# Reciprocal standard deviation of a node update: square root on ScalarE and a Newton step on VectorE in place of GpSimd's power

## The reference, cut to what matters

```
y = concatenate(h, agg);  x1 = x + h + silu(y @ uW1 + ub1) @ uW2 + ub2
h2 = (x1 - mean(x1)) / sqrt(var(x1) + 1e-5)
logits = h2 @ router_w.T            # top 2 of 8 experts, softmax, shares
out = x1 + h2 + sum of share * expert(h2)
```

## Time and profile before

| what | value |
|---|---|
| median of 3 runs | 2668.64 us (2668.3 to 2669.28) |
| the profiled execution's own time | 2669.72 us |
| its span in the profile | 2668.0 us |
| busy share of the span: PE, PEld, DVE, ACT, POOL | 76, 70, 79, 63, 66% |
| ACT_TABLE_LOAD instructions on ACT | 4, one each at L506, L1095, L1549, L1915 |
| the update's first instructions, last send | 2149.95 us, 2379.46 us |

### The profile page before, as it was taken

How to read it: one execution, slowest core, us unless ns; L and a number is a source line. 1 busy time by engine, 2 the same in 40 slices (tenths; PEclk the granted TensorE clock), 3 DMA queues, 4 the chain that set the end, 5 groups by cost and what they waited for, 6 DMA issues and landing times. The chain is left out here.

```text
span 2668.0 us, 63199 instructions
## 1 busy us (share of the span) xinstructions
PE 2024.5 (76%) x14160; PEld 1864.0 (70%) x14161; DVE 2099.9 (79%) x6765; ACT 1692.9 (63%) x3817; POOL 1769.8 (66%) x2247
## 2 busy tenths in 40 slices
PE   0000595009999999999999999999999979829980
PEld 0000584008999999999999999999999857719980
DVE  9994474028999999999999999999999837736766
ACT  5340121027888888888888888888888735418860
POOL 0007777738887878878878788788788715755660
PEclk9999998558999999999999999999999989959995
DMA  5000243012222222222222222222222354444548
GB/s 162 0 0 9 73 144 94 6 37 76 72 72 71 73 71 71 74 71 71 73 72 72 73 70 73 71 71 74 71 71 73 65 172 128 143 127 132 155 134 290
DMA packets 145565, 230.56 MB, mean 86 GB/s; under 512 B 33241, under 2 KB 101491, under 8 KB 145214
## 3 DMA queue, kind: packets, MB, share of 16 engines
q0 software_dynamic: 60672, 139.93, 18.0%
q1 hardware_dynamic: 75758, 81.69, 10.2%
q10 hardware_dynamic: 9040, 7.85, 0.9%
HBM read 167.41 MB, written 61.73 MB: 86 GB/s over the span
## 5 line engine op out<-in xcount | busy, mean ns | idle before, releaser
L1035 POOL DMA_INDIRECT rows<-b_rows,dst_row x838 | 841.9, 1005 | 229.9 <-issue 146.7
L1162 PE MATMUL ps_z<-w_hi,t_hi 128*128 128x256 f32 x1676 | 547.3, 327 | 0.0
L1149 PE MATMUL ps_agg<-rows,onehot 128*126 128x256 f32 x1676 | 453.8, 393 | 19.6 <-DVE node_rows L1184 16.6
L1163 PE MATMUL ps_z<-w_lo,t_hi 128*128 128x256 f32 x1676 | 468.3, 279 | 0.0
L1164 PE MATMUL ps_z<-w_hi,t_lo 128*128 128x256 f32 x1676 | 467.9, 279 | 0.0
L1068 ACT ACTIVATE rows<-rows,shift,rstd_m 128x256 f32<-128x256 f32 x838 | 452.5, 587 | 0.0
L1184 DVE TENSOR_TENSOR node_rows<-node_rows,ps_agg 126x256 f32 x838 | 345.2, 412 | 105.5 <-issue 88.6
L460 POOL DMA_INDIRECT sorted_edges<-pay,place x245 | 241.9, 987 | 279.3 <-DVE place L802 199.5
L1095 ACT ACTIVATE rows<-rows 128x512 f32<-128x512 f32 x419 | 265.0, 632 | 188.4 <-DVE rows L1240 181.8
L1149 PEld LDWEIGHTS ps_agg<-rows,onehot 128*126 128x126 f32 x1676 | 281.3, 187 | 75.6 <-DVE node_rows L1184 25.3
L1045 POOL TENSOR_TENSOR rstd_m<-mv_m,half_m 128x2 f32<-128x2 f32 x419 | 307.2, 733 | 34.9
(11 more groups left out here) (316 smaller groups left out, 4366.3 us busy)
## 6 DMA issues: line engine op xcount, KB each, us to landing
x_e<-by_expert SPq DMA_DIRECT2D x56, 260.0 KB, 2.9
rows<-b_rows,dst_row POOLq DMA_INDIRECT x838
y_back<-y_rows SPq DMA_DIRECT2D x49, 252.0 KB
b_rows<-b_out SPq DMA_DIRECT2D x50, 126.0 KB
u_rows<-u_out SPq DMA_DIRECT2D x50, 126.0 KB
xh_rows<-xh_out SPq DMA_DIRECT2D x50, 126.0 KB
u_row_up<-u_rows SPq DMA_DIRECT2D x50, 126.0 KB
xh_row_up<-xh_rows SPq DMA_DIRECT2D x50, 126.0 KB
```

Of the source, the lines that this page charges most:

```text
L1035: nc.gpsimd.indirect_dma_start(rows[r][:, i, :], None, dram["b_rows"], bass.IndirectOffsetOnAxis(ap=dst_row[:, r, i:i + 1], axis=0)).then_ ...
L1149: mm = pe.matmul(ps_agg[0:BIN, i * D:(i + 1) * D], onehot[:, q, i, 0:BIN], rows[q][:, i, :], start=True, stop=True)
L1162: pe.matmul(z, t_hi[:, k, i, c, :], w2_hi[:, c, :], start=(c == 0), stop=False)
L1163: pe.matmul(z, t_hi[:, k, i, c, :], w2_lo[:, c, :], start=False, stop=False)
```

## The change

POOL's two operations per pair of bins go. ACT takes the square root of variance plus epsilon in the same even step, after its Silu, with epsilon as a bias that POOL sets once. DVE makes the reciprocal of the root and refines it by one Newton step, five chained operations, in the odd step before the normalization that uses it. `mv` keeps the variance without epsilon, so the one later use (`gain`) adds it.

```
-            nc.gpsimd.memset(half[:], -0.5).then_inc(consts, 1)
+            nc.gpsimd.memset(eps[:], LN_EPS).then_inc(consts, 1)
...
-            def normal(g):
-                hold(pool, stats_ready, g + 2)
-                nc.gpsimd.tensor_scalar(mv[0:BIN, g:g + 2, 1], mv[0:BIN, g:g + 2, 1], 1.0, LN_EPS, ALU.mult,
-                                        ALU.add).then_inc(eps_added, 1)
-                pool.wait_ge(eps_added, g // 2 + 1)
-                nc.gpsimd.tensor_tensor(rstd[0:BIN, g:g + 2], mv[0:BIN, g:g + 2, 1], half[0:BIN, :], ALU.pow
-                                        ).then_inc(rstd_ready, 1)
...
             for n in range(STEPS):
-                if due(n - 6) and n % 2 == 0:
-                    normal(n - 6)
...
                     nc.scalar.activation(act1[0:BIN, g % R, :], act1[0:BIN, g % R, :], ACT.Silu
                                          ).then_inc(silu_ready, 1)
+                g = n - 6
+                if due(g) and g % 2 == 0:
+                    if g == 0:
+                        act.wait_ge(consts, 12)
+                    act.wait_ge(stats_ready, g + 2)
+                    nc.scalar.activation(root[0:BIN, g:g + 2], mv[0:BIN, g:g + 2, 1], ACT.Sqrt, bias=eps[0:BIN, 0:1]
+                                         ).then_inc(root_ready, 1)
...
+            def normal(g):
+                y, var = rstd[0:BIN, g:g + 2], mv[0:BIN, g:g + 2, 1]
+                a, b = newton[0:BIN, 0, :], newton[0:BIN, 1, :]
+                dve.wait_ge(root_ready, g // 2 + 1)
+                then(nc.vector.reciprocal(y, root[0:BIN, g:g + 2]))
+                then(nc.vector.tensor_tensor(a, y, y, ALU.mult))
+                then(nc.vector.scalar_tensor_tensor(out=b, in0=var, scalar=LN_EPS, in1=a, op0=ALU.add, op1=ALU.mult))
+                then(nc.vector.tensor_scalar(a, b, -0.5, 1.5, ALU.mult, ALU.add))
+                nc.vector.tensor_tensor(y, y, a, ALU.mult).then_inc(rstd_ready, 1)
...
                 g = n - 7
                 if due(g):
+                    if g % 2 == 0:
+                        normal(g)
                     dve.wait_ge(rstd_ready, g // 2 + 1)
...
-            then(nc.vector.tensor_tensor(gain[0:BIN, :], mv[0:BIN, :, 1], rstd[0:BIN, :], ALU.mult))
+            then(nc.vector.scalar_tensor_tensor(out=gain[0:BIN, :], in0=mv[0:BIN, :, 1], scalar=LN_EPS,
+                                                in1=rstd[0:BIN, :], op0=ALU.add, op1=ALU.mult))
```

More of the change, by code:

```diff
@@ L1273, in update @@
         rstd = sb("rstd_u", [P, BINS])
-        half = sb("half_u", [P, 2])
+        eps = sb("eps_u", [P, 1])
+        root = sb("root_u", [P, BINS])
+        newton = sb("newton_u", [P, 2, 2])
         blank = sb("blank", [P, E, 2, XROW])
@@ L1322, in update @@
         stats_ready = sem("stats_ready")
-        eps_added = sem("eps_added")
+        root_ready = sem("root_ready")
         consts = sem("consts_u")
```

## The result

The median goes from 2668.47 us (4 runs, 2664.75 to 2669.28) to 2681.76 us (4 runs, 2680.26 to 2683.56): 13.3 us slower, a ratio of 1.0052, with a 95% interval of 1.0041 to 1.0064.

What follows compares the result with a forecast made beforehand. PE's order and its waits for ACT and DVE were taken to bound the stage; 19.3 us lost less 7.6 from POOL gave 11.7 on 2669.7, 2681.4 profiled, so 2680 median. Own range 2674 to 2690, widened to 2669 to 2693.

Steps and rivals of the forecast that it cites:

- What bounds the stage: Update loop: PE's order and its waits for ACT's `agg_t`/`act_t` and DVE's normalization, 0.27 us to spare, set the step.
- ACT's part: ACT: 47 more table loads of about 1.3 us; `agg_t` 0.3 us late, 0.8 in 16 steps with a weight copy.
- The load back: ACT, odd step: load before Silu, which ends 2.64 us after `agg_t` began; next `agg_t` wanted at 2.93, so covered.
- the rival of 2711: ACT: each table switch costs twice the load, 2.7 to 3.2 us a pair, giving 2711 us; chance 0.07.
- DVE's part: DVE, odd step: five chained operations take 1.05 us (0.85 to 1.3), so `ps_ht` comes 0.78 us late.
- Both meet in one step: Odd steps: PE waits for the later delay, not the sum; 18.3 us for 23 pairs plus 1.0 in routing steps, 19.3.
- What POOL gives back: Relief from POOL's dropped work in landing-row waits, tail and final sends: 7.6 us together.
- The 2.0 for landing rows: Loop: ACT's waits for first sends to land before renaming rows vanish; 2.0 us of their 6.4 counted.
- The tail's relief of 3.0: Tail steps: waits for POOL's power and the rename go, two Newton chains and a load come; 3.0 us net, 1 to 5.
- for that I had 2.6: End of stage: POOL would owe no sends beyond the 25 after the last batch of five is placed; 2.6 us gained.
- The sum: Whole kernel: 19.3 - 7.6 = 11.7 us on the profiled 2669.7, giving 2681.4; median predicted 2680.

Runs made afterwards that it cites:

- no_switch_ht: Changed kernel with Identity for Sqrt on ACT, Newton chain kept, and PE's transposition of the normalized rows one step later: 2670.86 us, ratio 1.0012.
- neither: Changed kernel with Identity for Sqrt on ACT and the reciprocal alone on DVE, so no table loads and no Newton step: 2668.41 us, ratio 0.9989.
- no_newton: Changed kernel with the reciprocal alone on DVE, without the four Newton operations; Sqrt and its table loads stay: 2682.24 us, ratio 1.0046.
- newton_twice: Changed kernel with a second Newton step on DVE, nine chained operations in place of five: 2709.5 us, ratio 1.0155.
- no_switch: Changed kernel with Identity in place of Sqrt on ACT, so no table load; the Newton chain on DVE stays: 2687.39 us, ratio 1.0059.

## Why the prediction came out, step by step

It said 2680.0 us, between 2669 and 2693; measured 2681.76.

**What bounds the stage** held. PE's order of work and the two results that it waits for, `act_t` and the normalized rows, decide, and idle time of ACT or DVE elsewhere in the step counts for nothing. no_switch_ht shows it from the other side: the same operations on DVE, with another place to be ready for, cost a fraction.

**ACT's part** held with small errors. 47 loads came, of 1.283 us, each switch without a standstill beside the load. Sqrt on two columns took 0.295 us, not the logits copy's 0.18. That makes `agg_t` 0.1 us later than I had said, 0.9 late in place of 0.8 in step 35, which follows a step of the kind that I had read. In most other steps behind a weight copy it is 1.15 late, as in the timeline above, because there `agg_t` is wanted 0.93 us after Silu's end and not 1.18 as in the earlier trace rows: I had priced 16 steps from one. The load back is hidden, as said: Silu ends 2.64 us after `agg_t` began (2300.51 to 2303.15), the figure of the prediction. The switch alone costs 13.0 us in 21 odd steps (84.58 against 71.54); by my lateness (15 with a weight copy at 0.8, 6 at 0.3) it would be 13.8.

The Trainium skill ("ScalarE: Activation LUTs", What ACT_TABLE_LOAD costs) states about 2.66 us for every switch, half of it a drain. The trace differs: from Silu's end to Sqrt's start, with the load between, it shows 1.30 us (2298.43 to 2299.73), and the measurement decides. By the page's figure the rival of 2711 would have been near; it is refuted.

**DVE's part** held: 0.97 us for the chain, where I had taken 1.05 between 0.85 and 1.3. Four more operations cost 0.80 more. The root is ready long before, as said.

**Both meet in one step** held, and is the step that carries the result: chain alone +18.6 us of loop (3.3 of it clock), switch alone +12.1, both +17.2 rather than 30.7. I had 18.3 for 23 pairs, 16.7 of it for the 21 whose odd steps lie in the loop, and 1.0 for routing steps; the odd steps measured +19.3 and the even ones -2.1. Behind a weight copy I had put the two delays 0.02 us apart; the chain is the longer in 9 of the 15 odd steps behind one.

**What POOL gives back** is the term that I mis-sized: 7.6 us predicted, and some 3.4 seen. Without chain and switch the medians leave 2.7 us (2671.14 to 2668.41). The 2.0 for landing rows came: the waits are gone from the loop, in after as in neither. Neither's whole loop of 144.4 us doesn't show it, since the clock fell in steps 11 and 12 and other odd steps are up to 0.2 us longer, but single steps do. In before ACT waits for landing rows in steps 27, 32, 37, 42 and 47; of the steps behind them, 33, 38, 43 and 48 take 3.53, 3.05, 3.52 and 3.35 us in before and 3.12, 2.67, 3.07 and 2.67 in neither, 1.9 us less, and 28 is unchanged. The tail's relief of 3.0 came to 0.7: in neither the tail is 3.3 us shorter than before's, in no_newton 3.1, and with the whole chain 0.7 (0.8 of what is missing is step 51, which I had among the pairs). And POOL still owed sends when the last batch of five was placed; for that I had 2.6, and 0.8 came. These are the places, and the last two sends (the code leaves 25 after the places):

```profile
2363.21 0.17 DVE L1683 CAST place_up<-place_f_up 126x10 int32<-126x10 f32 x1
...
2396.30 0.99 POOL L1447 DMA_INDIRECT by_expert<-node_rows,place_up  x1 [0.30 <-issue]
2397.59 1.14 POOL L1447 DMA_INDIRECT by_expert<-node_rows,place_up  x1 [0.30 <-issue]
```

That is 35.5 us where 25 sends at 1.29 make 32.3: some two sends were owed, as before (in both traces 27 sends start behind the places). I had said that POOL, freed and in longer steps, would owe none. But POOL can send only what has been placed: the batch ahead of it was placed at 2351.99, 11.2 us earlier, and the ten sends that this released, from 2352.99 on, take 12.9; ahead of them POOL had stood idle for 4.75 us. In the tail the places come faster than the sends, whatever POOL did earlier. The counter-example is newton_twice: with its tail 4.0 us longer, only the 25 sends start behind the places, and they take 34.2 us.

**The sum** was 2681.4 for the profiled execution, which took 2683.56. By stretches, my sum makes 15.7 us for the loop (16.7 and 1.0, less 2.0), 0.8 for step 7 ahead of it, and 0.8 less 5.6 for tail and sends, with step 51. Measured are +17.2 in the loop, +2.4 from the start up to step 8, and -1.5 in tail and sends: 6.4 us more than I had said. Stretches that I hadn't reckoned with took 4.2 off again: the experts' span is 2.9 shorter and the rest 1.3. Over the ten traces step 8 starts anywhere from 2182.6 to 2187.6 and the experts' span lies between 183.8 and 188.6, with no order by kernel that I can see. So the agreement to 2 us is in good part luck; what the prediction got right is the mechanism of the loop, and its size to 1.5 us.

## What to carry to other kernels

Before work moves to an engine that is half idle, find the place that it gets in that engine's stream and what stands right behind it: a table load ahead of Silu cost nothing here, while one ahead of the copy that PE waits for cost up to 1.04 us a step (step 49, 4.77 us in no_newton against 3.73 in neither). Where two delays end at the same wait, the longer one is the price: removing either alone shows little, so test both alone and neither. And relief for an engine that feeds the end of a stage is worth only what its last pieces of work, which are released late, allow. Before a single long step is explained by a wait, look at the granted clock in it.

## What the runs showed of the hardware that was not expected

A table load starts as soon as the activation before it ends (0.01 us behind it here) and doesn't wait for its own activation's input: in step 38 the load began at 2298.44, while DVE wrote the statistics that Sqrt reads until 2298.70. What hides a load is slack on either side of its activation. In the earlier trace rows it ran while the input was being made. Before the Silu of step 39 it ran from 2301.44 to 2302.72, though the input was there at 2300.65, and cost nothing, since PE wanted the result only at 2304.22 (`ps_st`). In the changed kernel no wait of PE is for the Silu behind the 23 loads, and the even steps are no longer than in before, but for 0.1 us in one.

TensorE's granted clock, 1.00 in the loop of before and after, fell in single steps of five other traces, as in step 21 of no_switch, where PE had waited 1.51 us; four matmuls of `ps_v` then took 2.04 us in place of 1.03.

A Sqrt of 126x2 with a bias took 295 ns, a copy of 126x8 150 to 180. A reciprocal of 126x2 took 149 ns against 466 for 126x50, no dearer than the multiplications beside it.
